# Where a comparison stands in a pipelined loop: the sum of exponentials and its test, one tile later

## The reference

```python
t = jnp.max(xx[:, None, :] + Wt[None, :, :], axis=-1) + bt   # max over d, per token and f
z = t[:, :, None]
cvx = jnp.max(z * sl_cvx[None] + of_cvx[None], axis=-1)
ccv = jnp.min(z * sl_ccv[None] + of_ccv[None], axis=-1)
trop = s * cvx + (1.0 - s) * ccv
fused = g * trop + (1.0 - g) * classical
out = fused @ Wd + bd
```

## Time and profile before

| | us |
|---|---|
| median of three runs (lowest, highest) | 7930.42 (7920.41, 7934.19) |
| the profiled execution | 7926.71 |
| its span | 7924.9 |
| first tropical pass, from its first one-hot to its last test | 3069 to 4615 |
| PE busy over the span | 6689.3 (84%) |
| DVE busy | 5805.8 (73%) |
| ACT busy | 3549.0 (45%) |
| POOL busy | 1831.1 (23%) |

### The profile page before, as it was taken

The page is one execution under the profiler, slowest core; times in us unless marked ns, Lnnn a source line. Parts: engine busy times, 40 slices in busy tenths (PEclk is TensorE's granted clock), DMA queues, the critical chain, the costliest instruction groups (busy, mean ns, idle before and its releaser), DMA issues. The chain is left out here.

```text
span 7924.9 us, 114293 instructions
## 1 busy us (share of the span) xinstructions
PE 6689.3 (84%) x31338; PEld 4475.2 (56%) x31338; DVE 5805.8 (73%) x11104; ACT 3549.0 (45%) x7012; POOL 1831.1 (23%) x3939
## 2 busy tenths in 40 slices
PE   7888899999988864888888868888767788878887
PEld 4444799999977753555555545554433333333333
DVE  5655333333368876888888889999978888888888
ACT  3333222222234433555555522222217677767776
POOL 2222000000024433555555520223640000000000
PEclk9999999999989987999999989999989999999999
DMA  2222000000035441111111110122441111111111
GB/s 86 80 81 84 25 0 0 0 0 0 0 101 155 152 130 64 66 65 66 64 67 64 67 41 26 60 74 98 158 160 51 59 72 56 56 56 71 59 56 43
DMA packets 319084, 517.20 MB, mean 65 GB/s; under 512 B 27617, under 2 KB 231778, under 8 KB 318946
## 3 DMA queue, kind: packets, MB, share of 16 engines
q1 hardware_dynamic: 286050, 400.32, 15.1%
q0 software_dynamic: 32896, 115.51, 4.3%
HBM read 293.94 MB, written 221.79 MB: 65 GB/s over the span
## 5 line engine op out<-in xcount | busy, mean ns | idle before, releaser
L1756 DVE SCALAR_TENSOR_TENSOR t_tout<-t_fetched,t_top,t_tout 128x1024 f32<-128x1024 f32 x896 | 1145.6, 1279 | 240.2 <-PE t_fetched L1671 230.6
L1671 PE MATMUL t_fetched<-t_wpart,t_onehot 128*128 128x512 f32 x4096 | 1181.1, 416 | 160.4 <-DVE t_tout L1756 142.9
L2023 PE MATMUL ts_fetched<-t_wpart,ts_onehot 128*128 128x512 f32 x3232 | 991.3, 434 | 163.0 <-DVE ts_tout L2099 107.1
L1671 PEld LDWEIGHTS t_fetched<-t_wpart,t_onehot 128*128 128x128 f32 x4096 | 700.7, 188 | 513.6 <-DVE t_tout L1756 341.6
L548 PEld LDWEIGHTS l_ps<-hx,l_whh 128*128 128x128 f32 x8192 | 962.5, 193 | 16.8 <-DVE hx L489 3.7
L548 PE MATMUL l_ps<-hx,l_whh 128*128 (+1 forms) x8192 | 950.5, 275 | 3.2 <-DVE hx L489 3.2
L2099 DVE SCALAR_TENSOR_TENSOR ts_tout<-ts_fetched,ts_top,ts_tout 128x1024 f32<-128x1024 f32 x716 | 919.2, 1284 | 26.7 <-PE ts_fetched L2023 0.4
L2441 PE MATMUL f_pso<-f_fused,f_wd 128*128 128x512 f32 x1024 | 588.0, 704 | 375.7 <-DVE f_fused L2513 375.7
L2525 DVE SCALAR_TENSOR_TENSOR f_line<-f_hinge,f_vec,f_line 128x512 f32<-128x512 f32 x1024 | 769.2, 751 | 126.2 <-ACT f_line L2405 98.6
L2023 PEld LDWEIGHTS ts_fetched<-t_wpart,ts_onehot 128*128 128x128 f32 x3232 | 574.9, 197 | 496.6 <-DVE ts_tout L2099 399.4
L513 ACT ACTIVATE l_act<-l_ps 128x128 f32<-128x128 f32 x1024 | 285.0, 278 | 1054.1 <-PE l_ps L548 1054.1
(11 more groups left out here) (371 smaller groups left out, 10995.0 us busy)
## 6 DMA issues: line engine op xcount, KB each, us to landing
t<-t_tout SPq DMA_DIRECT2D x128, 512.0 KB, 2.6
f_t<-t SPq DMA_DIRECT2D x32, 2048.0 KB, 10.1
g_adj<-in_adj SPq DMA_DIRECT2D x128, 256.0 KB, 3.1
g_adjt<-in_adjt SPq DMA_DIRECT2D x128, 256.0 KB, 3.3
t_x<-x_normalised SPq DMA_DIRECT2D x130, 128.0 KB, 2.4
g_x<-in_x SPq DMA_DIRECT2D x64, 256.0 KB, 2.9
x_kept<-g_x SPq DMA_DIRECT2D x64, 256.0 KB, 2.2
g_x<-x_kept SPq DMA_DIRECT2D x64, 256.0 KB, 2.8
```

The costliest lines, as they stand in the source:

```text
L1671: mm = pe.matmul(fetched[c % RING][:, h * CH:(h + 1) * CH], one_hot[g][:, c % GRP * P:(c % GRP + 1) * P], w_part[part][:, k, h * CH:(h + 1 ...
L1756: dve.scalar_tensor_tensor(t_out[j][:, :], column[:, :], value, t_out[j][:, :], ALU.add, ALU.max)\
L2023: mm = pe.matmul(fetched[buf][:, h * CH:(h + 1) * CH], one_hot[b][:, c % GRP * P:(c % GRP + 1) * P], w_part[part][:, k, h * CH:(h + 1) * C ...
```

## The change

`add_up` and `test` of a tile run one slot later. On PE, `add_up(s - 2)` stands between the second and third fetch of slot s, where `add_up(s - 1)` stood behind the sixth. On DVE, `test(s - 2)` stands between candidates five and six of slot s, where `test(s - 1)` closed the slot. Since they begin at s = 2, the first four slots are written out instead of the first two, and the last ones are caught up in `last()`. ACT, POOL and SP keep their order and their waits; only `begin`'s wait is written with `wait_past` for the unrolled slots.

```diff
         def tiles(eng, slot, last):
 
-            for s in range(2):
-                slot(s, s)
-            with eng.Fori(1, TILES // 2) as i:
+            for s in range(4):
+                slot(s, s % 2)
+            with eng.Fori(2, TILES // 2) as i:
...
             def begin(s, j):
 
                 act.wait_ge(fetched_ready, s * CANDS + 1)
-                if not isinstance(s, int):
-                    act.wait_ge(t_stored[j], (s - j) * 8)
+                wait_past(act, t_stored[j], (s - j) * 8)
...
             def slot(s, j):
-                before = not isinstance(s, int) or s > 0
                 spread(s, j, 1)
-                for c in range(4):
+                for c in range(2):
                     fetch(s, c)
-                if before:
+                if not isinstance(s, int) or s > 1:
+                    add_up(s - 2, j)
+                for c in range(2, 4):
+                    fetch(s, c)
+                if not isinstance(s, int) or s > 0:
                     turn_fall(s - 1)
                 for c in range(4, 6):
                     fetch(s, c)
-                if before:
-                    add_up(s - 1, 1 - j)
                 spread(s + 1, 1 - j, 0)
                 for c in range(6, 8):
                     fetch(s, c)
 
             def last():
+                add_up(TILES - 2, 0)
                 turn_fall(TILES - 1)
                 add_up(TILES - 1, 1)
...
                 name(s + 1, 1 - j)
-                for c in range(4, CANDS):
+                for c in range(4, 6):
                     use(s, j, c)
-                if not isinstance(s, int) or s > 0:
-                    test(s - 1, 1 - j)
+                if not isinstance(s, int) or s > 1:
+                    test(s - 2, j)
+                for c in range(6, CANDS):
+                    use(s, j, c)
 
             def last():
-                test(TILES - 1, 1)
+                for j in range(2):
+                    test(TILES - 2 + j, j)
```

## The result

The changed kernel takes 8154.09 us (median of four runs, 8151.49 to 8157.34) and the kernel before, on the same chip, 7929.78 (7920.41 to 7934.19): ratio 1.0285, 95% interval 1.0267 to 1.0303. It is slower by 224 us. The prediction was 8162, range 8108 to 8285. The profiled execution's span grew from 7924.9 to 8151.4 us.

A forecast was written before the change was run, and what follows sets the result against it. It took a loop of waits, with no engine full, to bound the kernel at 12.02 us a tile. Terms 205 (loop) + 1 (end) + 26 (clock) = 232 us gave 8158.7, median 8162 us, range 8108 to 8285.

The forecast's parts named there:

- The loop, 13.66 us: First pass: a tile's loop through DVE's late test, ACT and PE's next fetch takes 13.66 us against 12.02, +1.64 a tile.
- U1 to T: On DVE, from a tile's first use to the end of the late test: 7.70 us.
- T to H: On ACT, from the late test's end through `allowed`, copy, counts and distance to the one-hot's end: 3.49 us.
- H to U1: From the one-hot's end through PE's fetch and ACT's first value to DVE's next first use: 2.47 us.
- The term of 205 us: Slots 3 to 127 of the first pass: 125 tiles at +1.64 us each, 205 us.
- Who waits: Waits a tile: `allowed` some 6.5 us, PE for the one-hot 2.3, POOL some 6.8, DVE before first use some 3.4.
- POOL's floor just below it, 13.46: POOL's own loop from the test to the lifted `y`, wanted by `best`, allows no tile below 13.46 us.
- The rival built on it, that POOL decides: If ACT is quicker than added up, POOL's loop sets the tile: 8111 to 8125 us; chance 0.10 (below 8120).
- The sum's move costs nothing: PE's sum before fetch 2 alone costs 0.23 us a tile, but is hidden in the longer loop.
- The clock, 26 us: PE's hole of some 2.3 us a tile lowers the granted clock for 6% of the pass: 26 us, bounds 0 to 171.
- The rival of a low clock in nearly every tile: PE's clock falls in nearly every tile of the first pass: 8307 us or less; chance 0.13 (8250 to 8320).
- Not slower: The test fills DVE's hole between uses five and six, gaining 15 to 49 us, about 7898; chance 0.04.

The follow-up runs named there:

- e6: Changed kernel with POOL's taking and next best ahead of `leave(s - 2)`, ACT as changed: 8148.5 us, ratio 1.0277 to the kernel before.
- e7: Changed kernel with `allowed` in two buffers and the next tile's `turn_hot` ahead of the counts on ACT, POOL as changed: 8149.2 us, ratio 1.0276.
- e1: Changed kernel with `allowed` in two buffers, so ACT's `fall_off` waits for an earlier test: 8140.0 us, ratio 1.0273 to the kernel before.
- e3: Changed kernel with the test behind use three instead of use five, the sum as changed: 7908.7 us, ratio 0.9981 to the kernel before.
- e5: Changed kernel with two buffers for `allowed`, `turn_hot` ahead of the counts on ACT, and next best ahead of `leave` on POOL: 7906.0 us, ratio 0.9971.
- e4: Kernel before with one move, `add_up(s - 1)` between fetches 4 and 5 instead of behind fetch 5: 7859.1 us, ratio 0.9916.
- e2: Changed kernel with the sum, for tile s-1, back behind fetch 5 and only the test late: 8573.1 us, ratio 1.0817 to the kernel before.
- e9: Kernel with two buffers for `allowed`, with PE's spread of group 1 done five times (sixteen more matmuls, same values): 8125.3 us, ratio 1.0248.
- e11: Kernel before with four slots of the first pass written out instead of two, on DVE alone: 7937.4 us, ratio 1.0008.
- e10: Kernel before with 48 one-element memsets more on DVE at the head of the first pass: 7923.2 us, ratio 0.9994.

## Why the prediction was right

**The loop, 13.66 us.** Measured 13.64 to 13.66. Its legs, by the timeline after: U1 to T 7.62 (forecast 7.70), T to H 3.46 (3.49), H to U1 2.51 (2.47). The term of 205 us is 125 tiles by 1.63, 204 us.

**Who waits.** `allowed` 6.7 us for the test (forecast 6.5); PE for the one-hot 2.4 (2.3); POOL 6.8 (6.8); DVE before U1 3.4 to 3.5 (3.4); the hole before use six gone; 0.29 us to spare for `best` (0.2). That it is ACT's chain and not POOL's that sets 13.64 is shown by e6 (POOL freed, 13.65) and e7 (ACT freed, 13.34).

**POOL's floor just below it, 13.46.** e1 and e7 have it at 13.34 to 13.37. The rival built on it, that POOL decides, falls with e6: freeing POOL doesn't move the tile (13.65).

**The sum's move costs nothing.** Right, and understated: with the sum in its new place the tile is 11.80 us in e3 and 11.73 in e5, against 12.02 before; e4 shows that PE's 0.78 us before fetch 6 is worth 64 us when it is moved one fetch, with the test in its old place, and e2 that the new place is needed once the test is late.

**The clock, 26 us: mis-sized.** Five tiles had low clock (14.88 to 16.40 us), 8.5 us in all. One of them in windows of the changed kernel (stretch, length, PE's busy time, granted clock, DMA share, GB/s):

```profile
4080.00:4084.00 4.00, 2.28 (x5) 0.60 0.55 191
4084.00:4088.00 4.00, 4.00 (x15) 0.55 0.02 6
4088.00:4092.00 4.00, 3.39 (x20) 1.00 0.00 0
```

PE is idle for 1.7 us in the first row, works through the second at the 1.2 GHz level for most of it, and has the full clock again in the third. The granted clock is down for most of the first row already, so it fell inside PE's hole. The step that failed was to take the second pass's share of 6% for this one. A hole of 2.4 us in every tile of 13.65 rarely met it; the shorter tiles of e1 and e7, with smaller holes, met it in 53 and 44 tiles (PE's longest wait is 1.3 us in e1, 1.7 in e7). The kernel before holds the opposite case in its second pass: in nine rounds in a row, some 13.7 us long, PE has one hole of 1.6 us each, and the clock fell once in each. Yet from 5120 to 5640, with 38 holes of 1.4 to 1.6 us, the mean is 0.97. The row of the nine rounds, as above:

```profile
5653.00:5766.00 113.00, 92.40 (x330) 0.87 0.52 172
```

So the hole's size doesn't tell how many tiles are hit; what does is open. The rival of a low clock in nearly every tile is refuted here; e2, with a mean of 0.86, is the kernel where it happens. The Trainium skill's page "TensorE: Matmul & The Clock Gate", section "HAM oscillation — how this bites in real kernels", has the clock fall anew in each round of a loop whose matmuls take less time than the wait behind them. Here PE works some 11 us between holes of 2.4, so that section doesn't describe this loop, and the prediction was wrong to draw its upper bound, 145 us more, from it. By this trace the clock fell in 5 of 125 tiles.

**Not foreseen: the feed-forward's 11.5 us.** The sum had no term for a stage whose code doesn't change. So two errors partly cancelled: 204 + 8.5 + 11.5 + 1.6 = 226 against 232. The loop was forecast to within 1%; that the whole time came within 8 us of the forecast is in part luck.

**Not slower.** This rival asked that ACT get from T to H within 1.3 us. It took 3.46. That there was something to gain is so: with both loops freed (e5) or the test two uses earlier (e3) the kernel is faster than before, by 24 and 15 us. That the gain comes from the test filling DVE's hole is not shown. In e3 and e5 the sum's move has closed that hole already (use six isn't held), and e4 gains 64 us by moving the sum alone.

## What to carry to other kernels

When the producer of a semaphore is moved later, list every engine that waits for it, and for each what stands behind that wait in its program order; a buffer that exists once ties the next tile to the last reader. Add up the loop through each waiter: if two are nearly equal, freeing one shows next to nothing, and only both together show what the wait costs. A wait that ends before the next engine asks is free (e3: 4.4 us a tile), so move the end of the wait before removing the wait.

## What the runs showed of the hardware

- The granted clock followed neither the length of the hole nor its presence in each tile: with 2.4 us holes in tiles of 13.65 us it fell in 5 of 125 tiles, with holes of at most 1.3 us in tiles of 13.36 us in 53 (e1), and 16 more matmuls a tile brought that down to 25 (e9). With holes of 1.6 us in the second pass of the kernel before it fell in nine rounds in a row, but seldom from 5120 to 5640, where the holes are as long.
- 34 more instructions in DVE's program, in a stage 1300 us earlier, brought 14 gaps of up to 1.7 us into the feed-forward and 7 us of length (e11), each gap just behind the start of an 8 KB packet of the `instruction` queue; 48 more memsets took 11 us off it (e10). A difference of 0.1% between two kernels can be this. Why the second shift shortens the stage is open.
